# A transformer block with mixture of experts: a plan of its own for the first turn, and the first sequence's softmax denominators by a product with ones

## Chip, cores and metric

The kernel runs on one core of a Trainium2 chip. The metric is the device time of one execution in microseconds (us); lower is better.

## What is computed

For 16 sequences of 512 tokens with 512 features: layer norm, attention with 16 heads of size 32, residual, then layer norm and a mixture of 32 experts (4 per token, with a capacity) beside a shared gated layer, residual. The part that matters here is the attention:

```python
kqv = x @ Wqkv + bqkv                       # x is the normed input
scores = jnp.einsum('bsnh,btnh->bnst', k, q) / math.sqrt(HEAD_SIZE)
scores = jnp.triu(scores) + -10000.0 * jnp.tril(ones, k=-1)
attn = jax.nn.softmax(scores, axis=2)
out = jnp.einsum('bnkq,bknh->bqnh', attn, v)
return out.reshape(b, s, NUM_HEADS * HEAD_SIZE) @ Wo + bo
```

## The kernel before

The work on sequences is a pipeline of 18 turns (`turns`, `turn`). In turn i TensorE projects sequence i to q, k and v, does the attention of sequence i-1, and the output product, router and shared layer of sequence i-2. Then a second phase runs the experts; the change doesn't touch it.

A turn is a row of numbered slots. Each engine walks through the same slots and issues in each what tables give it; slots set the order within an engine's queue only, and semaphores do the waiting between engines. The dense groups of a turn (`GROUPS`, `GROUPS_1` for turn 1 and so on) are lists of (kind, number, slots), where "none" leaves slots free. In turn 0 only q, k, v and the transposes xT of the next sequence exist, and it uses the general list `GROUPS` of 126 slots.

Attention goes by head groups (4 heads each, four groups hg 0 to 3 per sequence) and fills: ten fills of one PSUM bank each cover a group's causal scores, with two banks in turn.

- `scores` (line 587, TensorE, tile scores) and `maxima` (line 1042, VectorE, tile junk and nmax): scores of each query row, and their row minimum of the negated scores. `S_AT` gives their slots: hg 0 of a sequence and 3 fills of hg 1 in the sequence's own turn, the other fills in the turn after it.
- `sums` (line 741, ScalarE): exponentials of junk with the row's maximum as bias, added up to the softmax denominators. 40 fills with 64 activations per sequence. `shift_exps` (746) and `inverses` (1058) correct and invert them.
- `maxima_T` (1052 to 1056, VectorE) and `place_maxima` (413, SyncE's queue): the maxima are transposed and copied by 4 DMAs as one more row into stack_q.
- `scores_T` (604, TensorE, tile scores_T), `exp` (731, ScalarE, into probs), `triangles` (1206, GpSimd), `values` (613, TensorE, 16 products with v into o_ps): the transposed scores, their exponentials, and the product with v.
- `spread_inverses` (1069), `denominators` (624, four TensorE transposes), `den_copy` (750, ScalarE), `normalise` (1075, VectorE): the inverted sums brought to the layout of o_ps and multiplied in.

stack_q and stack_k hold q and k with heads on the right partitions. They are filled by SBUF-to-SBUF DMAs, twelve of 64 KB for each of q and k and each half (two head groups), all on SyncE's queue (`stack`, line 427). `scores` of hg 0 waits for the 24 DMAs of the first half.

Before the turns and in turn 0 the weights are split in two halves of 16 bit (`weights_hi`, 789, ScalarE; `weights_lo`, 1153, VectorE). `SPLIT_SLOT` gives the slots of the last five. The bias of v goes through Wo into bo: VectorE spreads it (1133, slot `BV_SPREAD`), TensorE multiplies in fp32 (`value_bias`, 521, `BV_PRODUCT`), VectorE adds (1136, `BV_ADDED`). `ROW_SLOT` gives the slots of four memsets of one row of stack_k (1138).

```python
S_AT = {1: (117, 120, 123, 2, 5, 8, 11, 14, 17, 20), 2: (23, 25, *range(31, 47, 2)), 3: (47, 49, 51, 53, *range(61, 73, 2)),
        0: (83, 91, 94, 96, 99, 101, 104, 107, 110, 113)}
SPLIT_SLOT = {slot: place for place, slot in zip(range(3, 8), (12, 22, 32, 42, 66))}
BV_SPREAD, BV_PRODUCT, BV_ADDED = 70, 80, 84
ROW_SLOT = {100 + 4 * hg: hg for hg in range(HG)}
```

Of the kernel before, what the change touches and what calls it, by code (L numbers as in the profile page):

```python
# [15 lines left out]
P = 128  # L16
# [49 lines left out]

GROUPS_1 = ([g for m in range(HG) for w in ("q", "k") for g in ((w, m, 4), ("none", 0, 4))]
# [20 lines left out]
class Plan:  # L88

    def __init__(self, groups, slots, bias_pace, route_pace, route_now, route_late, scatters):  # L90
# [15 lines left out]


PLAN = Plan(GROUPS, 126, 3, 1, ROUTE_NOW, range(1, 1 + 2 * (ROUTE_STEPS - ROUTE_NOW), 2), {0: range(61, 109, 3)})
PLAN_1 = Plan(GROUPS_1, 126, 3, 1, 0, (), {})
PLAN_16 = Plan(GROUPS_16, 126, 3, 1, ROUTE_STEPS, range(1, 1 + 2 * (ROUTE_STEPS - ROUTE_NOW), 2), {0: range(31, 63, 2), 1: range(74, 122, 3)})  # L110
PLAN_17 = Plan(GROUPS_17, 0, 1, 3, ROUTE_STEPS, (), {})


def plan_of(i):
    return {1: PLAN_1, BATCH: PLAN_16, BATCH + 1: PLAN_17}.get(i, PLAN) if isinstance(i, int) else PLAN

# [7 lines left out]
S_AT = {1: (117, 120, 123, 2, 5, 8, 11, 14, 17, 20), 2: (23, 25, *range(31, 47, 2)), 3: (47, 49, 51, 53, *range(61, 73, 2)),  # L124
        0: (83, 91, 94, 96, 99, 101, 104, 107, 110, 113)}
S_SLOT = {slot: (hg, f) for hg, slots in S_AT.items() for f, slot in enumerate(slots)}
EXP_SLOT = {slot + 1: at for slot, at in ST_SLOT.items()}
MAX_SLOT = {slot + 1: at for slot, at in S_SLOT.items()}
NM_SLOT = {slot + 2: hg for slot, (hg, f) in S_SLOT.items() if f == FILLS - 1}
assert max(max(MAX_SLOT), max(NM_SLOT)) < 125  # L130
# [6 lines left out]

SUM_SLOT = {slot + 1: at for slot, at in MAX_SLOT.items()}
SHIFT_SLOT = {slot + 2: hg for slot, hg in NM_SLOT.items()}
INV_SLOT = {slot + 5: hg for slot, hg in NM_SLOT.items()}  # L140
# [19 lines left out]
STAT_SLOT = {slot: t for t, slot in enumerate((90, 93, 96, 99))}  # L160
LN1_SLOT = {slot + 10 - t: t for slot, t in STAT_SLOT.items()}

SCALE1_SLOT = {slot + 2: t for slot, t in STAT_SLOT.items()}
# [141 lines left out]
def sequences(nc, a, c, ps, begin, ahead):  # L305
    with ExitStack() as ctx:
# [82 lines left out]
        def score_group(i, hg, proj, attn, f=FILLS):  # L389

            if hg == 0 or (hg == 1 and f < S_EARLY):
                return (i, hg) if proj else None
            return (i - 1, hg) if attn else None

        @block.sync
        def _(sp):
# [26 lines left out]
            def stack(name, n, half):  # L423

                groups, part = slice(half * SHG, (half + 1) * SHG), {"q": (0, 1, 0), "k": (0, 0, 1)}[name][n]
                for h in range(GH):
                    sp.dma_start(c["stack_" + name][n * HD:(n + 1) * HD, groups, h, :],
                                 c["split_" + name][part][h * HD:(h + 1) * HD, groups, :]).then_inc(stacked[half], 16)
# [17 lines left out]
            def turn(i, par, proj, attn, fin, nxt):  # L446
# [21 lines left out]
                if proj:  # L468
                    stack_ready(i, 1)
                    for n in range(3):  # L470
                        stack("q", n, 1)
# [4 lines left out]
                for t in range(1, TT):  # L476
                    if proj:
                        stack("k", t - 1, 1)
# [34 lines left out]
        def _(pe):  # L513
# [103 lines left out]
            def denominators(s, hg):  # L617
# [3 lines left out]
                pe.wait_ge(den_spread, n + 1)  # L621
# [39 lines left out]
        def _(act):  # L661
# [1007 lines left out]
```

## Time and profile before

| | |
|---|---|
| median of 3 runs | 2376.11 us (2374.84 to 2382.54) |
| profiled execution | 2375.91 us, span 2374.2 us |
| TensorE busy | 2172.2 us, 91% of the span |
| ScalarE busy | 1634.9 us, 69% |
| VectorE busy | 1532.0 us, 65% |
| GpSimd busy | 1119.2 us, 47% |

Busy time is the time in which an engine had an instruction at work; matmuls are pipelined, so a busy TensorE is not one at its peak. The span is that of the profiled execution on the device. In the rows below PE is TensorE, PEld its weight loads, DVE VectorE, ACT ScalarE, POOL GpSimd, SP SyncE (SPq its DMA queue). L604 is line 604 of the kernel. "idle before" is the time that the engine stood still ahead of an instruction, with what released it. Granted clock 1.00 is TensorE at 2.4 GHz, 0.50 at 1.2 GHz.

### The profile page before, as it was taken

The numbers are of one execution on the slowest core, as the hardware profiler recorded it, in microseconds if no ns is written. First come the engines' busy times: TensorE is split into PE (matmuls) and PEld (weight loads), VectorE is DVE, ScalarE is ACT, GpSimd is POOL, SyncE is SP. The second block draws the span as 40 slices with busy tenths as digits, with TensorE's granted clock in tenths as the row PEclk, the third lists the DMA queues.
The fourth block names the chain that finished last, engine by engine and source line by source line (L and its number), as shares of the span: only waits on it lengthen the run. The fifth ranks groups of instructions, "written<-read, shape, count | busy, mean of one in ns | idle before, by whom it ended". The sixth has DMA issues, their size and how long they took to land. (4 is left out here: it accounts for less than half of the span.)

```text
span 2374.2 us, 42120 instructions
## 1 busy us (share of the span) xinstructions
PE 2172.2 (91%) x13868; PEld 1135.9 (48%) x13868; DVE 1532.0 (65%) x5008; ACT 1634.9 (69%) x4025; POOL 1119.2 (47%) x1558
## 2 busy tenths in 40 slices
PE   7678999999999999999999999999998886999997
PEld 3234444444444444444444444444443444666664
DVE  4645667676757666767676767676666654667764
ACT  5687676777777777676867677777676623666664
POOL 3224143444444444444444444444442635777885
PEclk9789999999999999999999999999999997999998
DMA  6022222222222222222222222222212025999996
GB/s 230 18 55 62 54 73 58 71 67 68 69 59 72 59 77 66 65 63 63 63 64 63 63 64 63 64 63 63 63 46 81 15 103 159 248 247 247 244 246 130
DMA packets 158362, 222.39 MB, mean 94 GB/s; under 512 B 37824, under 2 KB 91168, under 8 KB 158144
## 3 DMA queue, kind: packets, MB, share of 16 engines
q1 hardware_dynamic: 129472, 177.58, 25.0%
q0 software_dynamic: 28672, 42.12, 8.7%
q8 instruction: 110, 1.80, 0.3%
q14 instruction: 108, 0.88, 0.1%
HBM read 112.65 MB, written 56.46 MB: 71 GB/s over the span
## 5 line engine op out<-in xcount | busy, mean ns | idle before, releaser
L741 ACT ACTIVATE junk<-junk,nmax 128x512 f32<-128x512 f32 (+3 forms) x1024 | 573.7, 570 | 157.4 <-DVE nmax L1042 155.2
L1042 DVE CUSTOM_DVE_ANT_0 junk<-scores,maskrow 128x512 f32<-128x512 f32 (+3 forms) x1024 | 464.8, 486 | 209.2 <-PE scores L587 181.4
L731 ACT ACTIVATE probs<-scores_T 128x512 f32<-128x512 f32 x640 | 375.4, 604 | 44.9 <-PE scores_T L604 44.8
L1206 POOL TENSOR_SCALAR_AFFINE_SELECT probs<-probs 128x256 f32<-128x256 f32 x512 | 195.6, 417 | 349.2 <-ACT probs L731 348.9
L1214 POOL DMA_INDIRECT slots_dram<-rec,idx x256 | 263.2, 1028 | 115.7 <-issue 105.6
L587 PE MATMUL scores<-stack_k,stack_q 96*128 96x512 f16 (+3 forms) x1024 | 249.8, 305 | 44.0 <-DVE nmax L1042 43.9
L604 PE MATMUL scores_T<-stack_q,stack_k 97*128 97x512 f16 (+3 forms) x1024 | 248.5, 305 | 38.3 <-ACT probs L731 33.8
L741 ACT ACTIVATION_READ_ACCUMULATOR junk<-junk,nmax 128x1 f32 x1024 | 212.3, 207 | 0.0
L1193 POOL TENSOR_TENSOR xres<-xres,bo 128x512 f32<-128x512 f32 x64 | 81.2, 1271 | 258.7 <-DMA xres<-in_x 258.7
L213 PE MATMUL dense<-xT_hi,wqkv_hi 128*128 128x512 f16 x512 | 197.6, 386 | 1.5 <-DVE xT_lo L1013 1.5
L215 PE MATMUL dense<-xT_hi,wqkv_lo 128*128 128x512 f16 x512 | 196.3, 383 | 0.0
L214 PE MATMUL dense<-xT_lo,wqkv_hi 128*128 128x512 f16 x512 | 196.2, 383 | 0.0
L1311 POOL DMA_INDIRECT out<-ex_y,ex_sidx x96 | 157.6, 1642 | 44.7 <-issue 24.7
L604 PEld LDWEIGHTS scores_T<-stack_q,stack_k 97*128 97x128 f16 x1024 | 92.7, 98 | 177.1 <-ACT probs L731 85.0
L587 PEld LDWEIGHTS scores<-stack_k,stack_q 96*128 96x128 f16 x1024 | 97.7, 100 | 156.1 <-DVE nmax L1042 65.8
L1013 DVE SCALAR_TENSOR_TENSOR xT_lo<-dense,xT_hi 128x512 f16<-128x512 f32 x128 | 87.8, 689 | 113.9 <-ACT xT_hi L670 113.8
L1199 POOL TENSOR_TENSOR split_q<-glu,split_q 128x512 f16<-128x512 f32 x64 | 77.0, 1202 | 176.8 <-ACT split_q L681 176.8
L1291 POOL DMA_INDIRECT ex_xg<-x2n_dram,ex_gidx x96 | 127.6, 1330 | 68.6 <-PE scores L1336 30.8
L613 PE MATMUL o_ps<-probs,v 128*32 128x512 f32 (+3 forms) x2048 | 151.1, 436 | 0.9 <-POOL probs L1206 0.9
L681 ACT ACTIVATE glu<-dense,bqk 128x512 f32<-128x512 f32 x128 | 89.5, 699 | 56.9 <-PE dense L215 55.0
L699 ACT ACTIVATE glu<-dense 128x512 f32<-128x512 f32 x64 | 38.7, 604 | 110.2 <-PE dense L215 110.1
L213 PE MATMUL dense<-sdT_hi,hT_hi 128*128 128x512 f16 x256 | 97.6, 381 | 17.8 <-DVE hT_lo L1034 17.6
(276 smaller groups left out, 5489.3 us busy)
## 6 DMA issues: line engine op xcount, KB each, us to landing
stack_q<-split_q SPq DMA_DIRECT2D x384, 64.0 KB, 2.0
stack_k<-split_k SPq DMA_DIRECT2D x384, 64.0 KB, 2.1
out<-xres SPq DMA_DIRECT2D x67, 256.0 KB, 3.2
x2n<-in_x SPq DMA_DIRECT2D x64, 256.0 KB, 3.1
xres<-in_x SPq DMA_DIRECT2D x64, 256.0 KB, 3.0
x2n_dram<-x2n SPq DMA_DIRECT2D x16, 1024.0 KB, 4.3
stack_q<-in_W_gate SPq DMA_DIRECT2D x16, 512.0 KB, 3.7
stack_q<-in_W_up SPq DMA_DIRECT2D x16, 512.0 KB, 5.4
```

Source lines behind the costliest of these rows:

```text
L213: pe.matmul(out, w[0], x[0], start=start, stop=False)
L214: pe.matmul(out, w[0], x[1], start=False, stop=False)
L215: return pe.matmul(out, w[1], x[0], start=False, stop=stop)
L587: last = pe.matmul(bank[:, at:at + cols], c["stack_q"][0:SROWS, hg, h, qt * P:(qt + 1) * P], c["stack_k"][0:SROWS, hg, h, 0:cols], start=T ...
L604: last = pe.matmul(bank[:, at:at + cols], c["stack_k"][0:SROWS + 1, hg, h, kt * P:(kt + 1) * P], c["stack_q"][0:SROWS + 1, hg, h, kt * P:k ...
L613: last = pe.matmul(bank[h * HD:(h + 1) * HD, kt * P:SEQ], loaded(kt, h), c["probs"][:, h, PCOL[kt]:PCOL[kt] + n], start=kt == 0, stop=kt = ...
L731: act.activation(to, at, ACT.Exp, scale=SCALE / (QS * QS)).then_inc(exp_done, 1)
L741: last = act.activation(x, x, ACT.Exp, scale=-1.0, bias=c["nmax"][:, hg % 2, m:m + 1], accum_out=c["sums"][:, hg % 2, m:m + 1])
L1042: last = dve.tensor_tensor_reduce(out=c["junk"][:, JUNK_AT[f], at:at + cols], in0=ps["scores"][f % 2][:, at:at + cols], in1=c["maskrow"][: ...
L1206: last = pool.affine_select(out=blk, in_=blk, compare_op=ALU.is_ge, fill=0.0, base=0, pattern=[[0, 2], [1, P]], channel_multiplier=-1)
L1214: pool.indirect_dma_start(out=a["slots"], out_offset=bass.IndirectOffsetOnAxis(ap=c["idx"][:, t, k:k + 1], axis=0), in_=c["rec"][:, t, k, ...
L1311: pool.indirect_dma_start(out=to, out_offset=bass.IndirectOffsetOnAxis(ap=e_["sidx"][q][:, ch:ch + 1], axis=0), in_=of, in_offset=None, co ...
```

## The change

1. Turn 0 gets its own plan, `PLAN_0` with the groups `GROUPS_0`: q and k of all head groups, v, 8 free slots, then xT with 2 free slots after each; 100 slots. Its score slots, `S_AT_0`, hold all 20 fills of hg 0 and hg 1 of sequence 0 (50, 52, ... 88), so turn 1 (`S_AT_1`) has the 7 late fills of hg 1 no more. The next sequence's norm statistics stand at slots 42, 46, 50, 54.
2. The weight splits move to slots 8, 15, 22, 29 and 92 (the last is the shared gate's), the spread of v's bias to 38, its product to 49, its sum to 53, the four row memsets to 4, 12, 32, 35.
3. In turn 0 the first half of stack_k is issued by ScalarE's queue (`first_keys`, slot 41, behind the second v eviction); SyncE's queue goes on with q's second half.
4. Sequence 0 has no `sums`, `shift_exps`, `inverses`, `spread_inverses`, `denominators` and `den_copy`. Instead TensorE does a second set of 16 products per head group, probs with a block of ones, right behind `values` (`probability_sums`, into the second scores_T bank), and VectorE divides (`divide`): transpose, reciprocal, copy over 32 rows, transpose back, multiply with o_ps. The first exponential of the next head group waits for the products.
5. Semaphore counts of the removed steps are shifted by one sequence. `counted` and `LINKS`, which no turn needs, are gone.

```diff
+GROUPS_0 = ([(w, m, 4) for m in range(HG) for w in ("q", "k")] + [("v", t, 4) for t in range(TT)] + [("none", 0, 8)]
+            + [g for t in range(TT) for g in (("xT", t, 1), ("none", 0, 2))])
...
+S_AT_0 = {(0, 0): tuple(zip(range(50, 70, 2), range(FILLS))), (0, 1): tuple(zip(range(70, 90, 2), range(FILLS)))}
+S_AT_1 = {at: slots for at, slots in S_AT.items() if at != (1, 1)}
...
+PLAN_0 = Plan(GROUPS_0, 100, 3, 1, 0, (), {}, S_AT_0, (42, 46, 50, 54))
+PLAN_1 = Plan(GROUPS_1, 126, 3, 1, 0, (), {}, S_AT_1)
...
-SPLIT_SLOT = {slot: place for place, slot in zip(range(3, 8), (12, 22, 32, 42, 66))}
-
-BV_SPREAD, BV_PRODUCT, BV_ADDED = 70, 80, 84
-ROW_SLOT = {100 + 4 * hg: hg for hg in range(HG)}
+SPLIT_SLOT = {slot: place for place, slot in zip(range(3, 8), (8, 15, 22, 29, 92))}
+
+BV_SPREAD, BV_PRODUCT, BV_ADDED = 38, 49, 53
+ROW_SLOT = {slot: hg for hg, slot in enumerate((4, 12, 32, 35))}
+
+KEYS_SLOT = 41
...
             def stacks(i):
                 stack_ready(i, 0)
-                for name in ("q", "k"):
+                for name in ("q",) if in_first(i) else ("q", "k"):
                     for n in range(3):
-                        stack(name, n, 0)
+                        stack(sp, name, n, 0)
...
+            def probability_sums(s, hg):
+
+                pe.wait_ge(exp_done, (s * HG + hg + 1) * FILLS)
+                columns(ps["scores_T"][1], lambda kt, h: c["ones"][:, 0:HD]).then_inc(den_done, 1)
...
                     if attn and slot in PV_SLOT:
                         values(i - 1, 1 - par, PV_SLOT[slot])
+                        if in_first(i - 1):
+                            probability_sums(i - 1, PV_SLOT[slot])
...
+                if f == 0 and 0 < s * HG + hg <= HG:
+
+                    act.wait_ge(den_done, s * HG + hg)
...
+            def first_keys():
+                act.wait_ge(qk_split, 2 * SHG)
+                for n in range(3):
+                    stack(act, "k", n, 0)
...
+            def divide(s, hg):
+
+                n = s * HG + hg
+                by_block = c["denT"][:, :].rearrange("p (n r) -> p n r", r=HD)
+                dve.wait_ge(den_done, n + 1)
+                dve.transpose(c["denT"][:, :], ps["scores_T"][1][:, :]).then_inc(den_read, 1)
+                dve.wait_ge(den_read, n + 1)
+                link(dve.reciprocal(c["rden"][:, hg, :], by_block[:, :, 0]))
+                link(dve.tensor_copy(by_block, c["rden"][:, hg, :].unsqueeze(2).broadcast_to([P, SEQ // HD, HD])))
+                need(dve, aT_ready, n)
+                link(dve.transpose(c["att"][:, :], c["denT"][:, :]))
+                dve.wait_ge(o_done, n + 1)
+                dve.scalar_tensor_tensor(c["att"][:, :], ps["o"][:, :], AS, c["att"][:, :], ALU.mult, ALU.mult).then_inc(att_done, 1)
```

How the order moves. ScalarE's queue in turn 0, from the v evictions on (x2n is the input's buffer, being normed), before:

```order
L688 ACTIVATE v<-dense 128x512 x3
L789 ACTIVATE sgT_hi<-xres 128x2048
L688 ACTIVATE v<-dense 128x512
L741 ACTIVATE junk,sums<-junk,nmax 128x512
L741 ACTIVATE junk,sums<-junk,nmax 128x128
L741 ACTIVATE junk,sums<-junk,nmax 128x384
L741 ACTIVATE junk,sums<-junk,nmax 128x512
```

and now:

```order
L703 ACTIVATE v<-dense 128x512 x2
L407 DMA stack_k<-split_k 32x2x512 x12
L703 ACTIVATE v<-dense 128x512 x2
L720 ACTIVATE x2n<-x2n,mv 128x512 x2
L685 ACTIVATE xT_hi<-dense 128x4x128
L720 ACTIVATE x2n<-x2n,mv 128x512
L685 ACTIVATE xT_hi<-dense 128x4x128
L720 ACTIVATE x2n<-x2n,mv 128x512
L685 ACTIVATE xT_hi<-dense 128x4x128 x2
L814 ACTIVATE sgT_hi<-xres 128x2048
L749 ACTIVATE probs<-scores_T 128x512 x2
```

The sums are gone up to the first exponentials of turn 1, the dozen DMAs stands between the v evictions, and the shared gate's split is last. TensorE in turn 1, around the product with v of head group 0, before:

```order
L624 MATMUL scores_T<-ident,att 128x128 x4
L587 MATMUL scores<-stack_k,stack_q 128x512
L613 MATMUL o_ps<-probs,v 32x512 x4
L613 MATMUL o_ps<-probs,v 32x384 x4
L613 MATMUL o_ps<-probs,v 32x256 x4
L613 MATMUL o_ps<-probs,v 32x128 x4
L213 MATMUL dense<-xT_hi,wqkv_hi 128x512
```

and now:

```order
L595 MATMUL scores<-stack_k,stack_q 128x512
L621 MATMUL o_ps<-probs,v 32x512 x4
L621 MATMUL o_ps<-probs,v 32x384 x4
L621 MATMUL o_ps<-probs,v 32x256 x4
L621 MATMUL o_ps<-probs,v 32x128 x4
L621 MATMUL scores_T<-probs,ones 32x512 x4
L621 MATMUL scores_T<-probs,ones 32x384 x4
L621 MATMUL scores_T<-probs,ones 32x256 x4
L621 MATMUL scores_T<-probs,ones 32x128 x4
L220 MATMUL dense<-xT_hi,wqkv_hi 128x512
```

The four transposes are gone and sixteen products with ones stand behind those with v. VectorE at the end of that head group, now:

```order
L1106 STREAM_TRANSPOSE denT<-scores_T 128x512
L1108 RECIPROCAL rden<-denT 128x16
L1109 COPY denT<-rden 128x512
L1111 STREAM_TRANSPOSE att<-denT 128x512
L1113 SCALAR_TENSOR_TENSOR att<-o_ps,att 128x512
```

These five stand where one TENSOR_TENSOR of 128x512 (line 1075) stood.

## Rows read from the trace of the kernel before

**Rows 1.** Windows by turn: us of stretch, busy us (instructions) per engine, clock, DMA share, GB/s

```profile
88.00:183.00 95.00, 72.46 (x433) 34.53 (x434) 46.16 (x178) 78.02 (x214) 25.65 (x52) 0.90 0.18 46
183.00:276.00 93.00, 90.20 (x561) 43.84 (x560) 52.59 (x188) 67.19 (x177) 30.82 (x57) 0.97 0.21 60
```

**Rows 2.** Windows of stretches inside turns 0 and 1, same columns

```profile
44.80:52.40 7.60, 7.60 (x36) 3.33 (x34) 0.00 (x0) 3.59 (x4) 0.00 (x0) 1.00 0.43 104
52.50:60.20 7.70, 4.69 (x7) 2.05 (x7) 3.00 (x5) 0.60 (x1) 0.00 (x0) 0.65 0.42 102
62.00:88.00 26.00, 10.64 (x37) 4.87 (x35) 22.76 (x62) 15.38 (x44) 4.20 (x12) 0.56 0.00 0
88.00:92.00 4.00, 3.82 (x12) 1.62 (x13) 0.46 (x2) 2.36 (x8) 0.00 (x0) 0.50 0.37 88
92.00:128.70 36.70, 28.29 (x164) 13.22 (x163) 16.65 (x69) 30.92 (x85) 11.67 (x18) 0.95 0.06 14
128.70:151.80 23.10, 18.78 (x120) 8.60 (x118) 10.41 (x45) 20.63 (x59) 6.46 (x14) 1.00 0.43 114
151.80:170.20 18.40, 13.45 (x84) 5.67 (x83) 10.53 (x35) 13.67 (x35) 6.02 (x17) 0.83 0.01 1
170.20:183.20 13.00, 8.33 (x61) 5.44 (x60) 8.11 (x28) 10.44 (x31) 1.49 (x4) 0.76 0.28 67
```

**Rows 3.** Timeline of TensorE: start us, us, engine, line, op, operands, idle before

```profile
55.56 6.71 PE L521 MATMUL o_ps<-probs,att 128*128 128x512 f32 x8 [3.01 <-DVE att L1133]
62.11 0.60 PE L587 MATMUL scores<-stack_k,stack_q 96*128 96x512 f16 x3
...
88.18 0.58 PE L604 MATMUL scores_T<-stack_q,stack_k 97*128 97x512 f16 x1 [0.72 <-DMA stack_q<-nmT]
```

**Rows 4.** Timeline of SyncE's DMA queue, same columns, up to turn 2

```profile
13.13 2.58 SPq L487 DMA_DIRECT2D denT<-in_router_wT  x1
...
44.80 7.62 SPq L427 DMA_DIRECT2D stack_k<-split_k  x12
...
84.42 2.46 SPq L413 DMA_DIRECT2D stack_q<-nmT  x4
...
131.34 7.71 SPq L427 DMA_DIRECT2D stack_q<-split_q  x12
...
170.20 8.91 SPq L427 DMA_DIRECT2D stack_q<-split_q  x12
179.16 2.49 SPq L413 DMA_DIRECT2D stack_q<-nmT  x4
```

**Rows 5.** The page's DMA issues: KB each, us from issue to landing

```profile
stack_k<-split_k SPq DMA_DIRECT2D x384, 64.0 KB, 2.1
```

**Rows 6.** Timeline of ScalarE: the eviction of the second v group

```profile
47.41 0.60 ACT L688 ACTIVATE v<-dense 128x512 f32<-128x512 f32 x1 [1.99 <-PE dense L215]
```

**Rows 7.** Groups by line, 62 to 88 us: count, busy us, mean ns, idle before

```profile
L1042 DVE CUSTOM_DVE_ANT_0 junk<-scores,maskrow 128x512 f32<-128x512 f32 (+3 forms) x20 | 9.3, 498 | 7.1 <-PE scores L587 7.0
...
L1138 DVE MEMSET stack_k<- 1x2048 f16 x4 | 7.1, 1765 | 1.9 <-issue 1.9
```

**Rows 8.** Groups by line, 88 to 170 us, same columns

```profile
L741 ACT ACTIVATE junk<-junk,nmax 128x128 f32<-128x128 f32 (+3 forms) x56 | 31.0, 560 | 0.4 <-DVE nmax L1042 0.2
...
L604 PE MATMUL scores_T<-stack_q,stack_k 97*128 97x512 f16 (+3 forms) x64 | 16.8, 329 | 16.4 <-ACT probs L731 15.6 <-DMA stack_q<-nmT 0.7
```

**Rows 9.** Timeline of TensorE: one head group's product with v

```profile
106.84 2.36 PE L613 MATMUL o_ps<-probs,v 128*32 128x512 f32 x32 [0.47 <-POOL probs L1206]
```

**Rows 10.** Timeline of VectorE in turn 1

```profile
101.60 0.42 DVE L1069 COPY att<-rden 128x512 f32<-128x512 f32 x1
...
111.05 0.68 DVE L1075 TENSOR_TENSOR att<-att,o_ps 128x512 f32<-128x512 f32 x1
...
111.84 0.25 DVE L1063 RECIPROCAL rden<-shift 128x16 f32<-128x16 f32 x1
```

**Rows 11.** VectorE's 32x32 transposes by source line: ns min/median/max

```profile
L1053 DVE STREAM_TRANSPOSE nmF<-nmax x5: 202/203/204, 84.0 to 177.3; 128x32 f32<-128x32 f32 x5
```

More of the change, by code:

```diff
@@ L88, with __init__ @@
 class Plan:
-    def __init__(self, groups, slots, bias_pace, route_pace, route_now, route_late, scatters):
+    def __init__(self, groups, slots, bias_pace, route_pace, route_now, route_late, scatters, scores=None, stats=(90, 93, 96, 99)):
         ends, at = {}, 0
@@ L105, in __init__ @@
         self.scatter = {slot: (m, n) for m, slots in scatters.items() for n, slot in enumerate(slots)}
[L108 to L115, printed above, removed]
+        self.scores = {slot: (back, hg, f) for (back, hg), slots in (scores or S_AT).items() for slot, f in slots}
+        self.maxima = {slot + 1: at for slot, at in self.scores.items()}
+        self.maxima_T = {slot + 2: (back, hg) for slot, (back, hg, f) in self.scores.items() if f == FILLS - 1}
+        self.sums = {slot + 1: at for slot, at in self.maxima.items()}
+        self.shift = {slot + 2: at for slot, at in self.maxima_T.items()}
+        self.inverses = {slot + 5: at for slot, at in self.maxima_T.items()}
+        self.stat1 = {slot: t for t, slot in enumerate(stats)}
+        self.scale1 = {slot + 2: t for t, slot in enumerate(stats)}
+        self.ln1 = {slot + 10 - t: t for t, slot in enumerate(stats)}
 QUARTER = (0, 30, 60, 90)
@@ L387, in in_first, with score_group, stack @@
             return isinstance(i, int) and i == 0
[L389 to L393, printed above, removed]
+        def score_group(i, back, hg, proj, attn):
+            if back:
+                return (i - 1, hg) if attn else None
+            return (i, hg) if proj else None
+        def stack(eng, name, n, half):
+            groups, part = slice(half * SHG, (half + 1) * SHG), {"q": (0, 1, 0), "k": (0, 0, 1)}[name][n]
+            for h in range(GH):
+                eng.dma_start(c["stack_" + name][n * HD:(n + 1) * HD, groups, h, :],
+                              c["split_" + name][part][h * HD:(h + 1) * HD, groups, :]).then_inc(stacked[half], 16)
         @block.sync
@@ L470, in turn @@
                     for n in range(3):
-                        stack("q", n, 1)
+                        stack(sp, "q", n, 1)
                 if fin:
@@ L641, in turn @@
                         scores_T(i - 1, *ST_SLOT[slot])
-                    if slot in S_SLOT:
-                        q, f = S_SLOT[slot]
-                        of = score_group(i, q, proj, attn, f)
+                    if slot in plan.scores:
+                        back, q, f = plan.scores[slot]
+                        of = score_group(i, back, q, proj, attn)
                         if of:
                             scores(*of, f)
-                    if attn and slot in DEN_SLOT:
+                    if attn and slot in DEN_SLOT and not in_first(i - 1):
                         denominators(i - 1, DEN_SLOT[slot])
@@ L762, in turn @@
                         exp(i - 1, *EXP_SLOT[slot])
-                    if attn and slot in READ_SLOT:
+                    if attn and slot in READ_SLOT and not in_first(i - 1):
                         den_copy(i - 1, READ_SLOT[slot])
@@ L1164, in _ @@
             chain["turn"] = chain["links"]
-            turns(dve, counted)
+            turns(dve, turn)
             for n, (name, _) in enumerate(WEIGHTS):
```

106 lines of the change are left out of this document (48 added, 58 removed).

## The prediction

> **What bounds the kernel now.** I read the windows by turn first: in turn 1 TensorE is busy for 72.46 of 95.00 us, in turn 2 for 90.20 of 93.00 [rows 1]. Turn 2 and the turns that repeat it are TensorE's, and the change leaves their instructions alone. So whatever turns 0 and 1 gain or lose should pass through as a shift, and only they have to be costed. Next I cut these two turns into stretches [rows 2], and for each asked which wait ends last.
>
> Turn 0 ends in a chain. The product for the value bias starts at 55.56 after 3.01 us of idle and takes 6.71 us; the first scores start at 62.11, right behind it; turn 1's first transposed scores start at 88.18 [rows 3]. They were released by the row of maxima that the DMA queue issued at 84.42 [rows 4]. Between 62 and 88 us VectorE is busy for 22.76 of 26.00 us and the granted clock is 0.56 [rows 2]: 13 fills of scores are worked off there, and VectorE is the engine they queue for. Four row memsets of 1.765 us stand among them [rows 7].
>
> Turn 1, first stretch (88.2 to 128.7): from 92.00 to 128.70 ScalarE is busy for 30.92 of 36.70 us, TensorE for 28.29 [rows 2]. Up to 170 TensorE idled 15.6 us on ScalarE's exponentials, while ScalarE spent 31.0 us on 56 activations of the row sums [rows 8]. The sums stand ahead of exponentials in its queue, so they are on the path. Second stretch (128.7 to 151.8): ScalarE 20.63 and TensorE 18.78 of 23.10 us [rows 2], with SyncE's queue issuing 24 stacking DMAs from 131.34 on [rows 4]. Third (151.8 to 170.2): TensorE 13.45, ScalarE 13.67 of 18.40 us [rows 2]. Last (170.2 to 183.2): SyncE's queue alone: 8.91 us for q, then 2.49 us for the maxima [rows 4], with TensorE busy for only 8.33 of 13.00 us [rows 2].
>
> **Turn 0, term by term.** (a) Splits, spread and row memsets move ahead of the scores. On VectorE they fall into time before the scores, and of its queue only four moved memsets (7.1 us in all, [rows 7]) leave the scores' stretch. I cost them at nothing in the new place: between 44.80 and 52.40 VectorE is busy for 0.00 us [rows 2]. If that cover were gone, the spread would come late and the bias product with it. The split of the shared gate's weights goes the other way, behind turn 0's fills: ScalarE, without sums, has no work there, and VectorE's half stands behind the last fill, before turn 1 has a fill for it (its first is at slot 23). Nothing too. (b) The bias product follows the last v group at 52.5 with no idle. There the granted clock was 1.00 before the idle and 0.65 across it [rows 2]; at the upper level 6.71 us become about 3.4, so it ends at 55.9. (c) The first half of stack_k goes to ScalarE's queue behind the second v eviction, 47.41 + 0.60 = 48.0 [rows 6]. No row shows a DMA issued there. The nearest is the same dozen on SyncE: 7.62 us, so 0.64 each [rows 4]; below it nothing speaks for less than that, above it stands 2.58 us for one issue among the weight loads [rows 4]. I take 0.64, since shape and size are the same: issued by 55.6, landed 2.1 us later [rows 5], 57.7. That and not the bias product ends last. Two v evictions and two norms wait behind these DMAs; they are needed first by the fourth fill, so this costs nothing.
>
> The DMA engines are busy for a share of 0.43 with one such stream [rows 2], so two streams for 4 us still fit. The Trainium skill, "DMA: Bandwidth & Descriptors", section "Issuing engines are not separate DMA queues", speaks against this term: starting DMAs from several engines saves only the sequencer's issue time, which it calls usually small beside the DMA. Here the row contradicts the "usually small": 7.62 us of issue stand against 2.1 us of landing. By that rule the term would be near nothing, the first scores would stay near 62, and the sum would end at 2364.
>
> (d) From 57.7 on there are now 20 fills, 32 instructions of line 1042. Twenty of them were busy for 9.3 us [rows 7], 0.465 each, so 14.9 us. Beside them VectorE does four copies of xT, the bias sum and a statistic (about 0.68 us each by [rows 10], 4.1 us), and one small transpose (0.2 us, [rows 11]): 19.2 us. ScalarE has no sums there. First transposed scores at 57.7 + 19.2 = 76.9; rounded 77.0, 11.2 us earlier than 88.18. The maxima of head group 0 are known after half of it, so their DMAs are hidden.
>
> **Turn 1.** (e) First stretch, 40.5 us before. ScalarE loses 17 of the fills' sums, some 27 activations of at least 0.55 us (15 us): it is no longer the bound. TensorE: busy 28.29, and 3.82 before 92 at a clock of 0.50, make 32.1 [rows 2]; seven fills of scores left for turn 0 (about 1.5) and one set of transposes (0.4) go, a set of ones products comes. It has the shape of the product with v, 2.36 us [rows 9]: 32.6. Waits stay, since an exponential still stands behind the two evictions of each projection group; I add 2.1. So 34.7: minus 5.8 us. (f) Second stretch. SyncE's queue has the maxima (2.5), 24 issues at 0.64 (15.4, and the pauses between: 16.1), landing 2.1 [rows 4, 5]: 20.7. TensorE has 18.78 minus 0.9 plus 2.36 = 20.2. Both close together give 21.0: minus 2.1. (g) Third stretch: its sums belong to the next sequence and stay. The ones product adds 2.36, the transposes' absence gives 0.4: plus 1.9. (h) Last stretch: SyncE's queue is unchanged, 13.0; the ones product falls into TensorE's free 4.7 us.
>
> (i) VectorE's division takes the place of one multiplication of 0.68 us: transpose, reciprocal 0.25, copy 0.42, transpose, multiplication 0.68 [rows 10]. A transpose of 128x512 is not in the trace. Below stands the copy of that size, 0.42; above, sixteen times the 128x32 one, 16 x 0.202 = 3.2 us [rows 11]. I take 0.68, the row of the same size that also reads PSUM: 2.7 us for the chain. For three head groups four dense pieces cover it (two for the third). In the last stretch the early fills queue behind it: plus 1.0. With 3.2 us per transpose it would be 5 us per group, of which I count 9 in all on the path.
>
> Sum of turn 1: -5.8 -2.1 +1.9 +1.0 = -5.0 us. With turn 0: -16.2 us. Against the profiled execution's 2375.91 us (span 2374.2) that is 2359.7; the median of the runs is 2376.11, 0.2 above, so I say **2360 us**.
>
> **Rivals.** *Turn 1 closes up more*: the leftover waits of (e) vanish and the stretches come down to TensorE's own work, 32.6, 20.2 and 15.5 us. That is 2.1 + 0.8 + 4.8 better, 7.7 us: 2352. For it speaks that ScalarE loses a third of its work; against it that two banks of transposed scores still alternate with an exponential between.
> *Turn 1 gains nothing*: the ones products (four times 2.36, 9.4 us) eat what the sums gave, because the waits of [rows 8] turn out to be the alternation itself: only the 11.2 of turn 0 and the 1.0 lost in (i), 2366.
> *The two queues share*: when ScalarE starts at 48.0, SyncE still has 7 of its dozen; 19 issues one after another at 0.64 end at 60.2, landed 62.3, 4.6 later than in (c): 2364. With dear transposes on top (9 us) 2373; either alone 2364 to 2369. Against: the share of 0.43.
> *Slower*: ScalarE's queue issues as slowly as SyncE's did among the weight loads, 2.58 us each [rows 4]: 31 us from 48.0, landed at 81.1. The scores start 23.4 us later than in (c), turn 1 at 100.4, 12.2 later than now; minus the 5.0 of turn 1 that is 2383. It decides from a landing at 73.9 on, that is 1.98 us per issue. Against: the rows of the same shape show 0.64 throughout.
> That the sums don't leave is excluded by the order of ScalarE's instructions.
>
> **Chances and range.** Forecast 0.60 (its own range 2355 to 2365), closing up 0.13, turn 1 without gain 0.12, sharing or dear transposes 0.11, slower 0.04. Low end: the closing-up case less 3 for its own spread, 2349. High end: 2369, dear transposes alone, plus 2 for the spread, 2371; both together and the slower case are left out. A measurement of this kernel can tell about 0.3%, 7 us, so faster means below 2369. Faster 0.60 + 0.13 + 0.12 + half of 0.06 (within the sharing case) = 0.88; same 0.08; slower 0.04.
>
> **What would show it.** The first scores near 57.7 and not behind the bias product; a granted clock near 1.00 during that product; first transposed scores near 77 and those of turn 2 near 167; ScalarE's DMAs 0.64 us apart; ones products of 2.36 us a set; the division's transposes below 1 us; turn 2 as long as before. If turn 1's first transposed scores come after 85, or turn 1 lasts longer than 94 us, the forecast is wrong, and the ScalarE queue or the ones products are the steps to look at.

## The result, and the profile after

| | before | changed |
|---|---|---|
| median | 2375.49 us (5 runs, 2367.02 to 2382.54) | 2362.07 us (5 runs, 2360.55 to 2363.47) |
| span of the profiled execution | 2374.2 us | 2359.1 us |
| TensorE, ScalarE, VectorE busy | 2172.2, 1634.9, 1532.0 us | 2174.4, 1599.5, 1535.3 us |

The ratio is 0.9947, with a 95% interval of 0.9925 to 0.997: faster by about 13 us. The forecast was 2360, its range 2349 to 2371. The total came out, but part of it came from other places than the sum had it.

The windows of the changed kernel: turn 0's end in two stretches, the first two of turn 1, then turns 1 and 2 whole (us of stretch, busy us and instructions of TensorE, its weight loads, VectorE, ScalarE and GpSimd, then granted clock, DMA share, GB/s):

```profile
51.40:55.00 3.60, 3.56 (x9) 1.29 (x7) 0.00 (x0) 0.57 (x2) 0.00 (x0) 1.00 0.55 133
55.90:74.70 18.80, 12.55 (x48) 4.97 (x49) 16.90 (x68) 6.60 (x9) 1.05 (x3) 0.70 0.06 15
74.70:110.30 35.60, 29.81 (x192) 14.00 (x190) 15.80 (x52) 18.84 (x33) 11.37 (x18) 0.97 0.07 16
110.30:130.90 20.60, 19.25 (x143) 8.97 (x141) 11.00 (x40) 8.54 (x16) 5.30 (x10) 1.00 0.36 82
...
74.70:167.30 92.60, 74.85 (x535) 35.27 (x533) 47.35 (x155) 49.28 (x105) 25.44 (x52) 0.92 0.18 45
167.30:260.30 93.00, 90.19 (x560) 43.83 (x559) 54.20 (x193) 69.55 (x185) 30.91 (x57) 0.97 0.21 59
```

Against [rows 1]: in turn 1 ScalarE's work falls from 78.02 to 49.28 us, and the turn still takes 92.6. Turn 2 is what it was, 90.19 busy of 93.00.

TensorE's timeline of the changed kernel (start us, us, engine, line, operation, operands, idle before and its releaser): the bias product, the first scores, the first transposed scores, then the last transposed scores of head groups 1, 2 and 3, and turn 2's first.

```profile
51.36 3.60 PE L529 MATMUL o_ps<-probs,att 128*128 128x512 f32 x8
55.87 0.61 PE L595 MATMUL scores<-stack_k,stack_q 96*128 96x512 f16 x3 [0.91 <-DMA stack_k<-split_k]
...
74.73 0.63 PE L612 MATMUL scores_T<-stack_q,stack_k 97*128 97x512 f16 x1
...
109.23 0.39 PE L612 MATMUL scores_T<-stack_q,stack_k 97*128 97x256 f16 x2 [1.05 <-ACT probs L749]
...
130.03 0.38 PE L612 MATMUL scores_T<-stack_q,stack_k 97*128 97x256 f16 x2
...
153.00 0.61 PE L612 MATMUL scores_T<-stack_q,stack_k 97*128 97x256 f16 x2 [0.86 <-ACT probs L749]
...
167.26 0.63 PE L612 MATMUL scores_T<-stack_q,stack_k 97*128 97x512 f16 x1
```

The same events of the kernel before, from the same view:

```profile
127.69 0.39 PE L604 MATMUL scores_T<-stack_q,stack_k 97*128 97x256 f16 x2 [1.75 <-ACT probs L731]
...
149.04 0.39 PE L604 MATMUL scores_T<-stack_q,stack_k 97*128 97x256 f16 x2 [0.36 <-ACT probs L731]
...
169.52 0.61 PE L604 MATMUL scores_T<-stack_q,stack_k 97*128 97x256 f16 x2 [0.85 <-ACT probs L731]
...
182.85 0.61 PE L604 MATMUL scores_T<-stack_q,stack_k 97*128 97x512 f16 x1 [3.36 <-DMA stack_q<-nmT]
```

With [rows 3] these give the whole account. Turn 0 is counted from the end of the last v group (before: 55.56 - 3.01 = 52.55; now 51.36, since the product follows at once).

| stretch | before | now | change | forecast |
|---|---|---|---|---|
| up to the end of the v groups | 52.55 | 51.36 | -1.2 | 0 |
| to the first scores | 9.6 | 4.5 | -5.1 | -4.4 |
| to turn 1's first transposed scores | 26.1 | 18.9 | -7.2 | -6.8 |
| turn 1, to the last of head group 1 | 39.5 | 34.5 | -5.0 | -5.8 |
| to the last of head group 2 | 21.3 | 20.8 | -0.5 | -2.1 |
| to the last of head group 3 | 20.5 | 23.0 | +2.5 | +1.9 |
| to turn 2's first | 13.3 | 14.3 | +0.9 | +1.0 |
| sum | | | -15.6 | -16.2 |

Each stretch of turn 1 is cut here at the last transposed scores of a head group, which lies 0.7 to 2.8 us ahead of the forecast's cuts; so what is given to one stretch or the next is uncertain by about that.

ScalarE's timeline, with the moved DMAs (ACTq is its queue):

```profile
46.39 7.99 ACTq L407 DMA_DIRECT2D stack_k<-split_k  x12
54.42 1.09 ACT L703 ACTIVATE v<-dense 128x512 f32<-128x512 f32 x2 [7.45 <-issue]
```

The timeline of VectorE and TensorE at the fourth head group, with its division:

```profile
160.86 2.33 PE L621 MATMUL scores_T<-probs,ones 128*32 128x512 f32 x32
...
163.26 0.72 DVE L1106 STREAM_TRANSPOSE denT<-scores_T 128x512 f32<-128x512 f32 x1 [2.09 <-PE scores_T L621]
164.01 0.25 DVE L1108 RECIPROCAL rden<-denT 128x16 f32<-128x16 f32 x1
164.30 0.43 DVE L1109 COPY denT<-rden 128x512 f32<-128x512 f32 x1
164.76 0.71 DVE L1111 STREAM_TRANSPOSE att<-denT 128x512 f32<-128x512 f32 x1
165.51 0.69 DVE L1113 SCALAR_TENSOR_TENSOR att<-o_ps,att 128x512 f32<-128x512 f32 x1
...
166.86 0.61 PE L595 MATMUL scores<-stack_k,stack_q 96*128 96x512 f16 x1 [3.14 <-DVE nmax L1067]
```

ScalarE issues a DMA every 0.67 us (7.99 / 12) and stands still for 7.45 us ahead of its third v eviction; the first scores wait 0.91 us for these DMAs. A set of ones products takes 2.33 us, a 128x512 transpose on VectorE 0.71.

### The profile page after: what moved, and what is told of

The parts are those of the page before. It is cut to its first block and busy times, and to the rows that moved or that the text cites. A ratio compares the mean times of both kernels' runs of the same rounds, so it can differ in the third digit from the quotient of the medians.

```text
span 2359.1 us, 42192 instructions
## 1 busy us (share of the span) xinstructions
PE 2174.4 (92%) x13980; PEld 1135.8 (48%) x13980; DVE 1535.3 (65%) x5004; ACT 1599.5 (68%) x3889; POOL 1121.5 (48%) x1558
## 5 line engine op out<-in xcount | busy, mean ns | idle before, releaser
L759 ACT ACTIVATE junk<-junk,nmax 128x512 f32<-128x512 f32 x960 | 538.1, 570 | 146.7 <-DVE nmax L1067 144.5
L749 ACT ACTIVATE probs<-scores_T 128x512 f32<-128x512 f32 x640 | 375.4, 605 | 54.4 <-PE scores_T L612 54.2
L759 ACT ACTIVATION_READ_ACCUMULATOR junk<-junk,nmax 128x1 f32 x960 | 199.2, 207 | 0.0
```

Source lines behind the costliest of these rows:

```text
L749: act.activation(to, at, ACT.Exp, scale=SCALE / (QS * QS)).then_inc(exp_done, 1)
L759: last = act.activation(x, x, ACT.Exp, scale=-1.0, bias=c["nmax"][:, hg % 2, m:m + 1], accum_out=c["sums"][:, hg % 2, m:m + 1])
```

## The experiments

In each trace I read three things: the end of the last v group, the first transposed scores of turn 1, and those of turn 2. The differences are "turn 0's tail" and "turn 1". They repeat to some tenths: two traces of the kernel before give a tail of 35.6 and 35.6 us and a turn 1 of 94.7 and 94.1; two of the changed kernel 23.4 and 23.4, and 92.5 and 93.0.

### e1: all stacking DMAs on SyncE's queue

```diff
-                for name in ("q",) if in_first(i) else ("q", "k"):
+                for name in ("q", "k"):
...
-                    if in_first(i) and slot == KEYS_SLOT:
-                        first_keys()
```

> The changed kernel, but with all 24 DMAs of the first half of stack_q and stack_k on SyncE's queue again (ScalarE issues none). Theory A (the ScalarE queue brings nothing; SyncE starts at 34.1, is done with 24 issues at about 50.5 and they have landed by 52.7, before the bias product ends at 55.0): first scores at 55.0 instead of 55.9, and about 1 us less in the span (2358). Theory B (the split over two queues is what brings the first scores forward, as term (c) of the prediction had it): first scores at 60 or later, span 2363 or more.

Measured: 2373.23 us, ratio 0.9949 (0.993 to 0.9969) to the kernel before on that chip (2385.44). Its TensorE and, below, SyncE's queue:

```profile
50.47 3.60 PE L529 MATMUL o_ps<-probs,att 128*128 128x512 f32 x8
53.90 0.60 PE L595 MATMUL scores<-stack_k,stack_q 96*128 96x512 f16 x3
```
```profile
33.20 8.39 SPq L407 DMA_DIRECT2D stack_q<-split_q  x12
41.63 7.62 SPq L407 DMA_DIRECT2D stack_k<-split_k  x12
49.36 7.63 SPq L407 DMA_DIRECT2D stack_q<-split_q  x12
```

Without ScalarE's queue the keys are issued by 49.25, earlier than by ScalarE (54.4), and the first scores stand right behind the bias product with no wait. The tail is 22.3 us against 23.4. So theory A holds: ScalarE's dozen DMAs bring nothing and, in the traces, cost 1.1 us. The timed runs are too coarse to show it.

### e2: the new plan with the row sums kept on ScalarE

```diff
-                        if of and not in_first(of[0]):
+                        if of:
                             sums(*of, f)
...
-                        if in_first(i - 1):
-                            probability_sums(i - 1, PV_SLOT[slot])
...
-                        (divide if in_first(i - 1) else normalise)(i - 1, ATT_SLOT[slot])
+                        normalise(i - 1, ATT_SLOT[slot])
```

> The new plan of turn 0 and ScalarE's stacking DMAs, but the first sequence's denominators by ScalarE's sums as before. Theory A (ScalarE's sums were on the path of turn 0's fills and of turn 1's first stretch): turn 0's fills are held by ScalarE (20 fills of about 0.88 us and four norms), first transposed scores near 79 to 80 instead of 74.7, turn 1 some 2 us longer than the 92.5 of the changed kernel; time near 2368. Theory B (the earlier start and the plan are all, the ones product and the sums cost TensorE and ScalarE the same): first transposed scores near 75, time 2361 to 2363.

Measured: 2377.53 us, ratio 0.9972 (0.9957 to 0.9986). First scores 55.92 as in the changed kernel, turn 1's first transposed scores at 77.88 (tail 26.5 against 23.4), turn 2's at 170.22: turn 1 takes 92.3 us against 92.5. Its windows from the first scores on:

```profile
55.90:77.90 22.00, 13.97 (x49) 5.41 (x50) 17.65 (x72) 19.54 (x62) 1.05 (x3) 0.59 0.07 15
77.90:170.20 92.30, 70.27 (x421) 32.96 (x419) 43.71 (x159) 74.68 (x196) 25.38 (x52) 0.91 0.17 43
```

Theory A holds in turn 0, where the sums cost 3.1 us: ScalarE is busy for 19.54 of 22.00 us. It fails in turn 1, which was to be some 2 us longer: over the whole turn the exchange of sums for ones products is worth nothing (by stretch, see e9).

### e3: only the ones products, with the old plan

```diff
-PLAN_0 = Plan(GROUPS_0, 100, 3, 1, 0, (), {}, S_AT_0, (42, 46, 50, 54))
+PLAN_0 = PLAN
...
-SPLIT_SLOT = {slot: place for place, slot in zip(range(3, 8), (8, 15, 22, 29, 92))}
-BV_SPREAD, BV_PRODUCT, BV_ADDED = 38, 49, 53
-ROW_SLOT = {slot: hg for hg, slot in enumerate((4, 12, 32, 35))}
+SPLIT_SLOT = {slot: place for place, slot in zip(range(3, 8), (12, 22, 32, 42, 66))}
+BV_SPREAD, BV_PRODUCT, BV_ADDED = 70, 80, 84
+ROW_SLOT = {100 + 4 * hg: hg for hg in range(HG)}
```

with e1's edit, and seven fills of head group 1 back in turn 1 (`PLAN_1`, not shown).

> Only the denominators by the ones product; plan, slots and queues of turn 0 as before. Theory A (most of the gain is turn 0's plan): first scores stay at 62, first transposed scores at 85 to 87, turn 1 at 92 to 93 us instead of 94.7, so time near 2370. Theory B (the sums were the main cost): turn 1 at 88 or below, time near 2365.

Measured: 2384.61 us, ratio 0.9998 (0.9983 to 1.0012): no difference. The tail is 32.5 us (35.6 before), turn 1 93.6 (94.4 on average before). Most of the tail's 3.1 us are the bias product's, which took another time at the same place, behind the same idle:

```profile
54.41 3.70 PE L529 MATMUL o_ps<-probs,att 128*128 128x512 f32 x8 [3.01 <-DVE att L1174]
```

Theory B (turn 1 at 88 us or below) is out; theory A fits turn 1 but had the first scores at 62, and they stand at 57.95 because of that product. The trace is of e3's fastest execution (2380.96 us), and turn 2 begins 5.3 us earlier in it than before (177.50 against 182.85), which the median doesn't show. Whether the product takes 3.70 us in most executions of e3 isn't known.

### e4: only the bias product and the memsets earlier

```diff
-SPLIT_SLOT = {slot: place for place, slot in zip(range(3, 8), (12, 22, 32, 42, 66))}
+SPLIT_SLOT = {slot: place for place, slot in zip(range(3, 8), (12, 22, 32, 42, 116))}
-BV_SPREAD, BV_PRODUCT, BV_ADDED = 70, 80, 84
-ROW_SLOT = {100 + 4 * hg: hg for hg in range(HG)}
+BV_SPREAD, BV_PRODUCT, BV_ADDED = 50, 67, 85
+ROW_SLOT = {slot: hg for hg, slot in enumerate((4, 12, 46, 48))}
```

In front of the last two memsets VectorE also waits for a weight split (not shown).

> The kernel before with only the weight splits, the bias spread and product and the four row memsets moved (product at slot 67, right behind the v groups; memsets before the scores; shared gate's split at slot 116). 13 fills in turn 0 and the sums as before. Theory A (the late bias product and the memsets were most of the 13 us): first scores near 56, first transposed scores at 75 to 77, turn 1 as before (94.7), time near 2364. Theory B (more fills in turn 0 without sums are needed for it): first transposed scores at 82 or later, time 2370 or more.

Measured: 2382.55 us, ratio 0.9983 (0.9971 to 0.9995), tail 28.2, turn 1 94.0. The first transposed scores, at 78.82, lie between the two theories (77 and 82). This run misled: besides what it was to test, it moved the shared gate's split to slot 116, ahead of the last fills. The trace shows VectorE's half of that split, 2.28 us, in front of the last fills' maxima, and TensorE idle for 7.10 us; e10, which differs in nothing else, has a tail 3.8 us shorter. VectorE and TensorE at the end of the tail:

```profile
75.47 2.28 DVE L1155 SCALAR_TENSOR_TENSOR sgT_lo<-xres,sgT_hi 128x2048 f16<-128x2048 f32 x1
...
78.42 0.61 PE L587 MATMUL scores<-stack_k,stack_q 96*128 96x512 f16 x1 [7.10 <-DVE nmax L1042]
...
78.82 0.63 PE L604 MATMUL scores_T<-stack_q,stack_k 97*128 97x512 f16 x1
```

### e5 and e6: both kernels again on another chip

No edit; the question was the bias product's length, and how far the traces repeat.

> The kernel before, unchanged, profiled once more. In the run with the ones product alone the bias product took 3.70 us behind the same 3.01 us of idle after which it took 6.71 us in the first profile of before. Theory A (whether TensorE's clock falls in that idle changes from execution to execution): this time product 3.7 us, first scores near 58, first transposed scores near 85, those of turn 2 near 178 to 179. Theory B (it falls always in the kernel before): 6.7, 62, 88 and 183 as in the first profile.

> The changed kernel, unchanged, on the chip of this group: ratio near 0.995, first transposed scores at 73 to 75, those of turn 2 92.5 us later. If theory A of the run of before holds, the gain read from traces of one chip is about 11 to 13 us and not 15.

Measured: the kernel before 2398.81 us in its single run, with the line

```profile
55.03 6.71 PE L521 MATMUL o_ps<-probs,att 128*128 128x512 f32 x8 [3.01 <-DVE att L1133]
```

so 6.71 us again, to the hundredth, and the first transposed scores at 87.65: theory B. The changed kernel: 2379.5 us, ratio 0.9937 (0.992 to 0.9954), product 50.49 for 3.60, tail 23.4, turn 1 93.0.

### e7: keys on SyncE's queue, and the fourth head group's division behind the early fills

```diff
-                    if attn and slot in ATT_SLOT:
+                    if attn and slot in ATT_SLOT and not (in_first(i - 1) and ATT_SLOT[slot] == HG - 1):
                         (divide if in_first(i - 1) else normalise)(i - 1, ATT_SLOT[slot])
+                    if attn and in_first(i - 1) and slot == 119:
+                        divide(0, HG - 1)
```

> The changed kernel with all stacking DMAs on SyncE's queue, and the division of the last head group moved from slot 117 to 119, behind the first early fill of the next head group. Theory A (in the last stretch TensorE waited 3.14 us for the fill's maxima, which stood behind the division): that wait goes, the last stretch is 13.0 to 13.3 us instead of 14.3, and with the earlier first scores the transposed scores of turn 2 come 2 us earlier than in the changed kernel; 2360 against 2362 on equal chips. Theory B (SyncE's queue bounds that stretch anyway): 14.3 stays.

Measured: 2382.3 us, ratio 0.9943 (0.9923 to 0.9963), beside 0.9937 for e6. In its trace the last stretch of turn 1 is 12.9 us (151.97 to 164.87; e6 has 13.5), and it ends in a wait of 2.07 us on the maxima's DMA where the changed kernel waits 3.14 us on VectorE. But e11, which has the same queue edit and the division in its place, has 13.1 us there, so moving the division is worth 0.2 us. Division and SyncE's queue end close to each other: taking away the one meets the other. The timed runs show none of it.

### e8: each set of ones products twice

```diff
-                columns(ps["scores_T"][1], lambda kt, h: c["ones"][:, 0:HD]).then_inc(den_done, 1)
+                columns(ps["scores_T"][1], lambda kt, h: c["ones"][:, 0:HD])
+                columns(ps["scores_T"][1], lambda kt, h: c["ones"][:, 0:HD]).then_inc(den_done, 1)
```

> The changed kernel with each set of products with ones done twice in a row (the second overwrites the first with the same values), four sets of 2.3 us more on TensorE. Theory A (TensorE is now what bounds turn 1's first three stretches): turn 1 grows by 2.3 for each of three sets, 6 to 7.5 us, the fourth is partly hidden. Theory B (TensorE waits for exponentials anyway, and the ones products fill these waits): turn 1 grows by less than 3 us.

Measured: 2386.62 us, ratio 0.9978 (0.996 to 0.9995). Turn 1 takes 100.7 us against 92.5 and 93.0: +7.9 for four more sets, and by head group, against the first trace, +2.7, +2.2, +2.2 and +1.1. Theory A: every set but the last stands on the path with its full 2.3 us. The timed runs agree: 7.1 us above e6 on the same chip (2379.5).

### e9: each set of ones products cut to four matmuls

```diff
-                columns(ps["scores_T"][1], lambda kt, h: c["ones"][:, 0:HD]).then_inc(den_done, 1)
+                for h in range(GH):
+                    last = pe.matmul(ps["scores_T"][1][h * HD:(h + 1) * HD, 0:P], c["ones"][:, 0:HD], c["probs"][:, h, 0:P], start=True, stop=True)
+                last.then_inc(den_done, 1)
```

This version leaves out most of the denominators of the first sequence; it only measures the time.

> The changed kernel with the ones product of each head group cut from 16 matmuls to 4 of 128 columns; it leaves out most of the denominators of the first sequence. Theory A, TensorE bounds turn 1 wherever the ones product stands: each set gives its 2.34 us back nearly whole, so turn 1 (first transposed scores to those of turn 2) goes from 92.5 to about 84.5 us in all, and the time to about 0.990 to 0.991 of the kernel before. Theory B, the banks of transposed scores and the exponentials bound turn 1: it stays at 90 us or more, and the ratio at 0.993 or above.

Measured: 2354.91 us, ratio 0.9928 (0.9905 to 0.9951). Its turn 1:

```profile
74.70:160.30 85.60, 66.93 (x438) 31.79 (x436) 47.70 (x155) 50.19 (x107) 25.37 (x52) 0.92 0.19 47
```

TensorE loses 7.9 us of work (74.85 to 66.93) and turn 1 shortens by 6.9 (92.5 to 85.6). By the trace this is theory A, whose 84.5 is missed by a microsecond; the ratio lies between the two theories (0.991 and 0.993) and its interval holds both. Dropping the sums was worth some 6.7 us in turn 1 (e2's 92.3 against 85.6), and the ones products take all of it back.

Turn 1 by stretch, in us:

| up to | before | e2 (sums) | changed (ones) | e9 (a fifth of the ones) |
|---|---|---|---|---|
| last of head group 1 | 39.5 | 37.8 | 34.5 | 32.5 |
| last of head group 2 | 21.3 | 21.4 | 20.8 | 18.9 |
| last of head group 3 | 20.5 | 20.5 | 23.0 | 21.5 |
| turn 2's first | 13.3 | 12.7 | 14.3 | 12.7 |

So the exchange isn't nothing everywhere. From e2 to the changed kernel it gains 3.3 and 0.6 us in the first two stretches, where the first sequence's sums stood, and loses 2.5 and 1.5 in the last two, which had none of them to lose but get a set of ones products each.

### e10: e4 again, with the weight splits where they were

```diff
-SPLIT_SLOT = {slot: place for place, slot in zip(range(3, 8), (12, 22, 32, 42, 116))}
+SPLIT_SLOT = {slot: place for place, slot in zip(range(3, 8), (12, 22, 32, 42, 66))}
```

> The kernel before with the value bias's spread, product and sum and the four row memsets moved ahead of the scores, and nothing else: the weight splits keep their slots, the shared gate's too. Theory A, early product and memsets are most of turn 0's gain, and the shared gate's split at a late slot was what held the earlier version of this up: first transposed scores at 74 to 76, ratio near 0.995. Theory B, the 7 fills that stay in turn 1 and the sums on ScalarE hold turn 0's end: first transposed scores at 79 or later, ratio near 0.998.

Measured: 2364.22 us, ratio 0.9961 (0.9948 to 0.9974) to 2373.83. TensorE:

```profile
50.55 3.60 PE L521 MATMUL o_ps<-probs,att 128*128 128x512 f32 x8
53.99 0.60 PE L587 MATMUL scores<-stack_k,stack_q 96*128 96x512 f16 x3
...
74.92 0.58 PE L604 MATMUL scores_T<-stack_q,stack_k 97*128 97x512 f16 x1
```

Theory A. The tail is 24.4 us: moving three numbers and four memsets gives 11.2 us in turn 0, with the sums on ScalarE, the old plan and the old queues. The changed kernel gains 12.2 there, with seven more fills in the stretch. Turn 1 stays at 94.2. In the timed runs e10 gains 9.6 us; e11, on the same chip, gains 13.1.

### e11 and e12: keys on SyncE's queue, and the bias product between the fills

e11 is e1 again. e12 adds to it:

```diff
-BV_SPREAD, BV_PRODUCT, BV_ADDED = 38, 49, 53
+BV_SPREAD, BV_PRODUCT, BV_ADDED = 38, {55 + 6 * k: k for k in range(DK)}, 86
...
-            def value_bias():
+            def value_bias(piece):
...
-                for k in range(DK):
+                for k in (piece,):
```

> The changed kernel with all stacking DMAs on SyncE's queue, once more, beside the next one. First scores at about 54, right behind the bias product. If the dozen DMAs on ScalarE's queue are worth nothing, the ratio to the kernel before is 0.993 to 0.995, no worse than the changed kernel's 0.9937 and 0.9947; if they are worth the 4 us that the prediction gave them, it is above 0.996.

> As the one before, and the value bias's product in four pieces behind the 3rd, 6th, 9th and 12th fill of turn 0 instead of ahead of the first. Theory A, the fills are VectorE's and TensorE has room between them: first scores at about 51.5 to 52 (the stacking DMAs landed), first transposed scores 2 us earlier than in the run beside it, ratio 0.001 lower if it passes through. Theory B, TensorE at its lower clock has no room there: each piece of 0.9 to 1.8 us holds up the next fill, and the first transposed scores are not earlier.

Measured: e11 2360.77 us, ratio 0.9942 (0.9924 to 0.996), tail 22.3, turn 1 91.8. e12 **2353.65 us, ratio 0.9912 (0.9894 to 0.9931)**, its slowest run (2354.62) ahead of e11's fastest (2355.01), and so the fastest version that computes the whole result. e12's TensorE:

```profile
51.80 0.61 PE L596 MATMUL scores<-stack_k,stack_q 96*128 96x512 f16 x3 [0.43 <-DMA stack_k<-split_k]
52.98 0.39 PE L596 MATMUL scores<-stack_k,stack_q 96*128 96x512 f16 x1 [0.58 <-DVE nmax L1066]
53.21 1.02 PE L529 MATMUL o_ps<-probs,att 128*128 128x512 f32 x2
...
69.65 0.38 PE L613 MATMUL scores_T<-stack_q,stack_k 97*128 97x512 f16 x1
```

The stretch from the first scores to the first transposed scores, e11 and then e12:

```profile
54.40:73.30 18.90, 13.12 (x50) 5.10 (x49) 16.85 (x68) 5.59 (x7) 1.05 (x3) 0.63 0.15 36
```
```profile
51.80:69.60 17.80, 11.94 (x56) 5.58 (x57) 16.05 (x65) 7.09 (x10) 1.05 (x3) 1.00 0.23 54
```

Theory A, by more than it said. Turn 1 begins 3.6 us earlier than in e11 (69.65 against 73.29): 2.6 because the first scores no longer stand behind the product, 1.0 because the stretch is shorter; 18.3 us of tail against 22.3. In that stretch the granted clock is 1.00 where e11 has 0.63, and TensorE's total falls from 13.12 to 11.94 us though the product is now in it.

## Why the prediction was right, and where its steps were wrong

The result lies in the range on the side that had most of the chance, and the sum of the trace (-15.6 against -16.2) is right partly by luck: turn 1 gave 2.1 us and not 5.0; 1.2 us that no edit made and 1.1 us more than forecast in turn 0's two last stretches made up for most of it; and the mechanism of (c) was wrong.

- **(a), (b)** Right in kind. The product starts where the v groups end, at clock 1.00, and takes 3.60 us (3.4 forecast). The moved work has cover. e10 shows that these two alone give 11.2 us in turn 0: 6.1 up to the first scores (9.6 to 3.4 us), 5.1 behind them, of the 7.1 us of memsets. Product and memsets moved together, so that division goes by stretch only. They are most of the change's gain. Of the 6.1, 3.0 are the idle and 3.1 the product's own length, 3.60 against 6.71; since e3 has 3.70 in the old place, this half may be smaller in other executions. In all ten traces with the product in one piece right behind the v groups it takes 3.60 us.
- **(c)** Wrong: ScalarE's queue was booked as what brings the keys in time. The price (0.67 a DMA; 0.64 forecast) and "ends last" were right, but the step that failed is that the keys needed help at all. [rows 4] had the answer: SyncE issued them at 44.80 for 7.62 us, so by 52.4, landed 2.1 us later at 54.5, ahead of the 55.9 at which the product was to end. Only the product held the first scores at 62.11. With the queue left alone (e1, e11) they come at once behind it; with ScalarE's they come 1.1 us later. The rivals on this term, the two queues sharing and the slower one, are out at 0.67 us a DMA. The Trainium skill's "DMA: Bandwidth & Descriptors", section "Issuing engines are not separate DMA queues", was right that the second issuer brings next to nothing here, though not for its reason: 8 us of issue are not small. The 2364 that I drew from it was wrong, since it left the first scores at 62.
- **(d)** 20 fills took 18.9 us, 19.2 forecast, and VectorE was busy for 16.90 of 18.80 us. Here the sums' absence pays: 3.1 us (e2). The forecast named that ScalarE has no sums there, and gave it no price.
- **(e), (f), (g)** Forecast -5.8, -2.1 and +1.9; measured -5.0, -0.5 and +2.5. Turn 1 gave 2.1 us (1.1 by e6 against e5) instead of 5.0. The ones sets had about the right price, 2.36 in each of these stretches: e8 and e9 show each on the path with nearly its whole length. What was mis-sized is what the absent sums set free: TensorE's waits were to shrink by 6.3 us in (e) (8.4 to 2.1) and by 3.5 in (f) (4.3 to 0.8). Windows from cut to cut, before and then changed:

```profile
88.18:127.69 39.51, 31.09 (x168) 14.19 (x168) 15.95 (x66) 32.09 (x88) 11.67 (x18) 0.90 0.09 21
127.69:149.04 21.35, 18.29 (x115) 8.33 (x116) 10.96 (x50) 19.69 (x60) 5.28 (x10) 1.00 0.34 78
```
```profile
74.73:109.23 34.50, 28.71 (x184) 13.34 (x182) 14.71 (x51) 17.80 (x32) 10.67 (x18) 0.96 0.07 16
109.23:130.03 20.80, 19.45 (x143) 9.14 (x144) 12.07 (x41) 8.90 (x16) 6.00 (x11) 1.00 0.32 77
```

  The waits shrank by 2.6 us (8.4 to 5.8) and by 1.7 (3.1 to 1.4). (e) still came out near its forecast, because TensorE's work, which was to rise by 0.5 us with the seven fills' absence counted in, fell by 2.4; beside it the granted clock is 0.96 where it was 0.90. That is luck in the size. The rival "turn 1 gains nothing" had the right reason for this, the ones products eating what the sums gave: over turn 1 e2 and the changed kernel are equal (92.3, 92.5). The 2 us that remain are the seven fills moved to turn 0 (94.2 in e10 to 92.3 in e2).
- **(h)** SyncE's queue in the last stretch is unchanged (8.68 for q, then 2.49), but the last ones set is not hidden, as the forecast had it: a second one adds 1.1 us there (e8), and cutting it to a fifth gives 1.5 back (e9).
- **(i)** The division's own costs were right: transposes 0.71 us each (0.68 forecast, bounds 0.42 and 3.2), the chain 2.9. The 1.0 us put on it was not its alone. The division begins when the ones set ends, and e9, which keeps the division and shortens the set, is down at 12.7 us like e2, which has neither; moving the division saves 0.2 (e7). The size of the stretch is uncertain too: 14.3, 13.5, 14.3, 13.1 and 13.1 us in the changed kernel, e6, e1, e11 and e12, against 13.3 and 12.8 in the two traces before, some 0.6 more on average.
- The 1.2 us before the v groups' end were no term, and no edit makes them: the changed kernel's own two traces have that end at 51.4 and 50.5. 0.5 us are there at the first projection (18.61 before, 18.11 now). Another 0.5 come from the clock: thirteen projection matmuls at the lower level, 0.43 us apart, before it rose, and eleven now, against 0.22 apart after. The 14th starts at 24.11 and 23.09. Over all 14 traces seven to thirteen are slow, and the v groups end at 50.5 to 52.6 accordingly. Why the clock rises earlier in one execution than in another is open.

The saving passed through the later turns only roughly: turn 2 begins 15.6 us earlier, the span of the profiled execution is 15.1 us shorter, and the timed runs give some 13. Which turns lose some of it changes from run to run (below).

## What to carry to other kernels

Before moving a transfer to a second queue, compare when it lands with when its consumer is otherwise free: here it landed before the product that really stood in the way. Work moved onto the engine that bounds a stretch is paid in full: here the ones products took 6.9 us in turn 1, where the sums that they replace had cost 6.7. Such an exchange pays only in the stretches where the work that goes away stood. And a long matmul whose result is needed late belongs between the small ones of a stretch that another engine bounds, not ahead of them: that gave 3.6 us in the first turns, and 7 in the timed runs beside e11.

## What the hardware showed that was not expected

- The same fp32 product, behind the same 3.01 us of idle, took 6.71 us in both traces of the kernel before and 3.70 in e3, whose granted clock over it is 1.00 where [rows 2] have 0.65. By windows of half a microsecond the clock fell some 2.3 us after the last v matmul in both traces of the kernel before (at 54.8 and 54.3) and did not fall in e3's idle of the same length. What differs between them ahead of it was not tried.
- Spreading the product between the fills (e12) kept the granted clock at 1.00 through a stretch in which e11 had 0.63, with less TensorE time in all. e11 and the changed kernel (0.70) had idle of about the same sum there.
- Turns with the same instructions differ by some 4 us with the clock. One turn of the changed kernel and the same turn of e12:

```profile
1125.20:1244.70 119.50, 112.24 (x700) 54.99 (x698) 77.70 (x281) 85.70 (x226) 52.15 (x85) 0.97 0.23 63
```
```profile
1118.90:1235.30 116.40, 109.36 (x700) 54.16 (x698) 77.34 (x281) 85.62 (x226) 52.08 (x85) 1.00 0.23 65
```

  In all 14 traces, cut at the one store of x2n that each turn makes (x2n_dram), the thirteen turns from the third on take 114 to 117 us at a clock of 1.00 and 117 to 120 at 0.97 to 0.99; which of them it hits is another in every trace, and no edit explains it. Within one chip this is the largest part of the scatter: the thirteen turns add up to 1508 to 1522 us over the eight traces of e1 to e8. It is also why e11's span is like the changed kernel's though its turn 2 began 2.2 us earlier: its thirteen turns took 1514.3 us, the changed kernel's 1512.0. e12's took 1509.1. Whether the further 3.5 us by which e12's median beats e11's, over its head start of 3.6, come from this or from its edit is open; but all five runs of e12 have a mean clock of 0.982, and e11's six have 0.977 to 0.980.
- The last turn, between the same cuts, differs by chip rather than by kernel: 99 to 106 us in the eight traces of e1 to e8, all on one chip, 88 to 91 in the other six, with the same kernel at 87.6 (changed) and 102.4 (e6). That is most of the 10 us and more by which the medians on that chip are longer. Its cause is open.
- Two queues that issue at once slow each other a little: SyncE's two dozens for q took 17.34 us beside ScalarE's dozen, and 8.39 and 7.63 us in e1, where the queue is alone; ScalarE's own took 0.67 us a DMA.
